# Third layer: mean first at the norms, reciprocal at once, bias columns two heads ahead, a values quarter in the first head

## What is computed

```python
def _cross_attention(q_in, kv_in, wq, bq, wk, bk, wv, bv, wo, bo, bias_k, bias_v):
    qh = (q_in @ wq + bq).reshape(b, q_len, H, K)
    kh = (kv_in @ wk + bk).reshape(b, t, H, K)
    vh = (kv_in @ wv + bv).reshape(b, t, H, K)
    kh = jnp.concatenate([kh, jnp.broadcast_to(bias_k, (b, 1, H, K))], axis=1)
    vh = jnp.concatenate([vh, jnp.broadcast_to(bias_v, (b, 1, H, K))], axis=1)
    logits = jnp.einsum('bqhk,bthk->bhqt', qh, kh) / scale
    weights = jax.nn.softmax(logits, axis=-1)
    ctx = jnp.einsum('bhqt,bthk->bqhk', weights, vh).reshape(b, q_len, H * K)
    return ctx @ wo + bo

res = x
h = _layer_norm(x, ln1_scale, ln1_offset)
x = res + _cross_attention(h, xf_1, wq1, ...)
res = x
h = _layer_norm(x, ln2_scale, ln2_offset)
x = res + _cross_attention(h, xf_2, wq2, ...)
h = _layer_norm(x, ln_mlp_scale, ln_mlp_offset)
h = jax.nn.gelu(h @ w_fc1 + b_fc1, approximate=False) @ w_fc2 + b_fc2
return x + h
```

## Time and profile before

| what | us |
|---|---|
| timed runs, median of 3 (lowest, highest) | 5109.34 (5104.77, 5110.42) |
| the profiled execution | 5106.48 |
| its span, first to last instruction | 5104.8 |
| busy in the span: TensorE, its weight loads | 4528.8, 3317.1 |
| busy: VectorE, ScalarE, GpSimd | 3084.9, 1932.5, 1675.9 |

### The profile page before, as it was taken

How to read it: one execution, slowest core, us unless ns; L and a number is a source line. 1 busy time by engine, 2 the same in 40 slices (tenths; PEclk the granted TensorE clock), 3 DMA queues, 4 the chain that set the end, 5 groups by cost and what they waited for, 6 DMA issues and landing times. The chain is left out here.

```text
span 5104.8 us, 72497 instructions
## 1 busy us (share of the span) xinstructions
PE 4528.8 (89%) x22864; PEld 3317.1 (65%) x22864; DVE 3084.9 (60%) x6414; ACT 1932.5 (38%) x3756; POOL 1675.9 (33%) x1119
## 2 busy tenths in 40 slices
PE   6999999578888888659999999998998999999996
PEld 3444444355666666448878778787787876877874
DVE  4555555147666666627677477575675756757642
ACT  2444444212222222125545245453354542545521
POOL 1222232235444444312323433323323234233240
PEclk8999988778888998779999999999999999999999
DMA  0000000200000000011211221211312112221123
GB/s 35 22 26 17 17 21 9 95 5 9 13 13 13 13 9 1 17 60 59 62 61 58 71 86 55 74 59 58 96 55 74 59 61 83 63 67 53 53 70 113
DMA packets 126288, 240.90 MB, mean 47 GB/s; under 512 B 16884, under 2 KB 38132, under 8 KB 124896
## 3 DMA queue, kind: packets, MB, share of 16 engines
q1 hardware_dynamic: 123744, 229.50, 14.2%
q0 software_dynamic: 2304, 8.39, 0.4%
HBM read 220.79 MB, written 16.78 MB: 47 GB/s over the span
## 5 line engine op out<-in xcount | busy, mean ns | idle before, releaser
L1786 POOL TENSOR_TENSOR c_wl<-c_wr,c_wh 128x512 fp32r<-128x512 f32 (+1 forms) x576 | 822.1, 1431 | 1744.8 <-ACT c_wh L2107 1531.7
L2199 ACT ACTIVATE c_pr<-c_ps,c_nms 128x257 f32<-128x257 f32 x512 | 245.3, 479 | 577.6 <-DVE c_nms L2389 575.1
L1355 POOL TENSOR_TENSOR b_sb<-b_sb,b_rt 128x1024 f32<-128x1024 f32 x128 | 285.0, 2227 | 490.1 <-DVE b_sb L1395 490.1
L572 ACT ACTIVATE a_ex<-a_ps 128x1024 f32<-128x1024 f32 x256 | 261.7, 1025 | 345.9 <-PE a_ps L408 345.6
L1395 DVE TENSOR_TENSOR_SCAN b_sb<-b_wt,b_s,b_ps 128x256 f32<-128x256 f32 x512 | 356.0, 732 | 11.7 <-issue 3.9
L1850 PE MATMUL c_ps<-c_hh,c_wh 128*128 128x512 f32 x768 | 319.4, 416 | 49.1 <-POOL c_hl L1792 49.1
L666 DVE TENSOR_REDUCE a_nm<-a_ps 128x2 f32<-128x1024 f32 x256 | 310.8, 1219 | 76.0 <-PE a_ps L385 73.0
L1850 PE MATMUL c_ps<-c_gh,c_wh 128*128 128x512 f32 x768 | 312.4, 407 | 41.9 <-DVE c_kl L2328 31.9
L2107 ACT ACTIVATE c_wh<-c_wr 128x512 fp32r<-128x512 f32 (+1 forms) x464 | 315.3, 685 | 9.6 <-PE c_ps L1852 8.5
L1852 PE MATMUL c_ps<-c_hh,c_wl 128*128 128x512 f32 x768 | 313.1, 408 | 0.0
L1851 PE MATMUL c_ps<-c_hl,c_wh 128*128 128x512 f32 x768 | 312.6, 407 | 0.0
(11 more groups left out here) (307 smaller groups left out, 11007.7 us busy)
## 6 DMA issues: line engine op xcount, KB each, us to landing
c_wr<-in_downs SPq DMA_DIRECT2D x192, 256.0 KB, 2.6
c_wr<-in_wv SPq DMA_DIRECT2D x64, 512.0 KB, 3.9
c_wr<-in_wk SPq DMA_DIRECT2D x128, 256.0 KB, 2.7
c_wr<-in_wq SPq DMA_DIRECT2D x128, 256.0 KB, 2.6
c_wr<-in_fc SPq DMA_DIRECT2D x64, 256.0 KB, 2.8
b_w<-in_w SPq DMA_DIRECT2D x8, 1024.0 KB, 13.5
a_x<-in_x SPq DMA_DIRECT2D x8, 512.0 KB, 3.4
a_ctx<-in_ctx SPq DMA_DIRECT2D x8, 512.0 KB, 4.1
```

What stands on the lines that cost most here:

```text
L572: act.activation(EX[:, n % 4, :, :], ps[:, BT + 2 * (n % 2):BT + 2 * (n % 2) + 2, :], ACT.Exp).then_inc(ex_ready, 1)
L1355: pool.tensor_tensor(SB[:, quad % 3, :, 0:L], SB[:, quad % 3, :, 0:L], RT[:, scan % 2, q // 4, :].unsqueeze(1).broadcast_to([P, 4, L]), AL ...
L1786: pool.tensor_tensor(piece(WL, slot), piece(WR, slot), piece(WH, slot), ALU.subtract).then_inc(piece_cut[slot], 1)
L2199: act.activation(PR[:, i, 0:L + 1], ps[:, BS + 1 - i % 2, 0:L + 1], ACT.Exp, bias=NMS[:, i:i + 1], scale=float(K2) ** -0.5, accum_out=RS[: ...
```

## The change

- *Norms.* TensorE: mean first, quarter 0, variance, quarters 1 and 2 (before: quarter 0, mean, quarter 1, variance, quarters 2 and 3). Quarter 3 stays in the norm only for attentions 2, 4 and 6 (`late_value` is true for 0, 1, 3, 5, 7); for the others it moves into head 0, between the next keys and queries and the transposes. VectorE: the reciprocal and the scaling come directly behind quarter 0, the low halves of quarters 1 and 2 behind the scaling. ScalarE: squares before the copy of quarter 0, the deviation before that of quarter 1, that of quarter 2 behind the high copies.
- *Columns.* `COL` has four slots instead of two, and the copy for head N + 2 is made in head N, behind the rows, instead of the copy for head N + 1 behind the softmax weights.
- *Ends of attentions.* `GL` of heads 0 and 1 is made by VectorE, one in head 14 and one in head 15, behind the rows, instead of both by GpSimd in head 14. TensorE's first output product waits for each of its banks just before it writes there, instead of for all three at first.
- *Feed-forward.* The next norm's reciprocals and scalings come one chunk earlier (after chunks 10 to 13 instead of 11 to 14).

```diff
-        COL = sb("col", [P, 2, 4])
+        COL = sb("col", [P, HSTEP, 4])
...
+        def late_value(t):
+
+            return t == 0 or t % 2 == 1
...
                 def head(h4, c, at=None):
                     u, v = c % 2, c // 2
-                    if at == H2 - 2:
-                        for m in range(2):
-                            pool.wait_ge(g_high, t * H2 + m + 1 + AHEAD)
-                            pool.sem_inc(passed, 1)
-                            pool.tensor_tensor(GL[:, m, :], G[:, m, :], GH[:, m, :], ALU.subtract).then_inc(g_low, 1)
...
             def gap(t, n):
 
-                if n == 0:
-                    pe.wait_ge(consts_in, 6 * 16 + AHEAD)
-                    pe.sem_inc(passed, 1)
-                    mean(n)
+                mean(n)
                 if t < B:
                     first_values(t, 0)
-                if n > 0:
-                    mean(n)
+                variance(n)
                 if t < B:
                     first_values(t, 1)
-                variance(n)
-                if t < B:
                     first_values(t, 2)
-                    first_values(t, 3)
+                    if not late_value(t):
+                        first_values(t, 3)
...
+                    if at == 0 and late_value(t):
+                        first_values(t, 3)
                     turn(N)
                     if at == H2 - 2:
 
-                        pe.wait_ge(v_low, t * H2 + H2 + AHEAD)
-                        pe.wait_ge(q_low, N + 2 + AHEAD)
-                        pe.wait_ge(k_low, N + 2 + AHEAD)
-                        pe.sem_inc(passed, 1)
                         down_ready(0)
-                        for d in (2, 0, 1):
+                        for d, free, count in ((2, v_low, t * H2 + H2), (0, q_low, N + 2), (1, k_low, N + 2)):
+                            pe.wait_ge(free, count + AHEAD)
                             add_down(0, DOWN_BANKS, 0, d, True)
...
                 act.wait_ge(g_used, used_count(last, 14) + AHEAD)
                 cut(1, count)
                 cut(0, count)
+                squares(n)
                 first_values(t, 0)
-                squares(n)
+                deviation(n)
                 first_values(t, 1)
-                deviation(n)
-                first_values(t, 2)
                 act.wait_ge(d_ps, n * EC + AHEAD)
                 act.sem_inc(passed, 1)
                 cut(3, count)
                 cut(2, count)
-                first_values(t, 3)
                 norm_high(n, range(EC))
+                first_values(t, 2)
+                if not late_value(t):
+                    first_values(t, 3)
...
-            def columns(N, index, u):
...
+            def columns(N, index, s):
-                dve.wait_ge(c_ready, N - 1 + AHEAD)
+                dve.wait_ge(c_ready, N - HSTEP + 1 + AHEAD)
                 dve.sem_inc(passed, 1)
-                dve.tensor_copy(COL[:, u, :], HC[:, index, :]).then_inc(col_ready, 1)
+                dve.tensor_copy(COL[:, s, :], HC[:, index, :]).then_inc(col_ready, 1)
...
             def gap(t, n):
-                first_values(t, 0)
                 centered(n)
                 if n % 3 == 1:
                     first_columns(t)
+                first_values(t, 0)
+                inverse(n, slice(0, N2))
+                scaled(n, range(EC))
                 first_values(t, 1)
                 first_values(t, 2)
-                inverse(n, slice(0, N2))
-                scaled(n, range(EC))
...
                             rows(N, t * (H2 // 2) + h4 * 2 + v, u)
+                            if at is None or at < H2 - 2:
+                                columns(N + 2, a * H2 + h4 * 4 + c + 2, (c + 2) % HSTEP)
+                            else:
+                                context_low(at - (H2 - 2))
...
                     if at != H2 - 1:
+                        queries(N + 1, (c + 1) % HSTEP)
                         if at != 0:
-                            columns(N + 1, a * H2 + h4 * 4 + c + 1, 1 - u)
-                        queries(N + 1, 1 - u)
-                        if at != 0:
-                            keys(N + 1, 1 - u)
+                            keys(N + 1, (c + 1) % HSTEP)
...
+                            if n == 10:
+                                inverse(b * 3 + 3, slice(0, L))
                             if n == 11:
-                                inverse(b * 3 + 3, slice(0, L))
+                                inverse(b * 3 + 3, slice(L, N2))
                             if n == 12:
-                                inverse(b * 3 + 3, slice(L, N2))
+                                scaled(b * 3 + 3, range(0, 2))
                             if n == 13:
-                                scaled(b * 3 + 3, range(0, 2))
-                            if n == 14:
                                 scaled(b * 3 + 3, range(2, 4))
```

More of the change, by code:

```diff
@@ L2420, in head, with context_low @@
                            .then_inc(pt_low, 1)
-                head_steps(t, dve, head)
-                for n in range(2, H2):
+                def context_low(n):
                     dve.wait_ge(g_high, t * H2 + n + 1 + AHEAD)
```

52 lines of the change are left out of this document (31 added, 21 removed).

## The result

The changed kernel takes 4966.55 us (median of 4 runs, 4958.13 to 4975.81) against 5108.73 (4 runs, 5104.77 to 5110.42) beside it: a ratio of 0.9723, 95% interval 0.9702 to 0.9744. It is 142 us faster; the forecast was 87, with a range down to 5000. The profiled execution took 4961.53 us with a span of 4959.9 (before: 5106.48 and 5104.8). The direction and the mechanism of most seams were right, the size was not: 55 us were missed, because the middle heads, held to be bound by TensorE, were not.

A forecast was written before the change was run, and what follows sets the result against it. The prediction took TensorE to bound the middle heads, so only seams could pay: 35 + 24 + 17 + 5 + 3 + 3 = 87 us, from 5106.5 to 5019.5 profiled, 5022 for the timed runs. The range was 5000 to 5056.

The forecast's parts named there:

- the first paragraph: Middle heads of an attention: bound by TensorE, busy 79.3 of 80 us, so only the seams can pay.
- G: Column copy in the 112 heads: 0.2 us on VectorE beside a never idle TensorE, so 0 gained.
- A: Heads 14 and 15 of the eight attentions: earlier low keys, part given back in head 15; 35 us gained.
- The third rival: Slower: the moved column copy meets GpSimd in every head, up to 128 us lost, total 5150; chance 0.03.
- the first rival: Head 15's late second low context brings half clock, so heads 14 and 15 gain 19 us, total 5038; chance 0.12.
- B: Norm between the two attentions of a pair, four times: mean first and an earlier reciprocal; 24 us gained.
- C: Norm before the feed-forward, three times: same steps with all four quarters kept; 17 us gained.
- F: End of the feed-forward, three times: scaling one chunk earlier frees VectorE for the last low half; 3 us gained.
- D: Start of the third layer, once: earlier deviation and cut, quarter 3 off the path to the first keys; 5 us.
- E: First three heads of the eight attentions: earlier columns gain 3 us in three, quarter 3 in head 0 nets 0 in five.
- The worst bound of the sum: Whole kernel: all bounds at their worst give 53 us gained, a total of 5056.
- What would show it: Profile signs: head 14's low-key wait gone, 1.5 to 2 in head 15, reciprocal 10.3 after mean, no ScalarE column waits.

The follow-up runs named there:

- experiment 7: The changed kernel with one VectorE instruction (low half of a values piece) made twice in heads 2 to 14, 0.75 us more a head: 4977.71 us.
- Experiments 1 and 2: 1: the kernel before with only the column copy changed, 5019.29 us; 2: the changed kernel with the column copy put back, 5041.5 us.
- 6: The kernel before with one VectorE instruction (low half of a values piece) made twice in heads 2 to 14, 0.75 us more a head: 5178.9 us.
- Experiment 8: The changed kernel with quarter 3 ahead of head 0's exponentials, the second low context ahead of head 15's rows, GpSimd's cuts behind the norm's low halves: 4957.87 us.
- experiment 12: The changed kernel with the two low contexts made by GpSimd again, bank-wise waits kept: 4971.16 us.
- Experiment 9: The changed kernel with only GpSimd's cuts moved behind the norm's low halves, in the seven norms that follow an attention: 4958.51 us.
- experiment 11: The changed kernel with quarter 3 in the norm for all eight attentions, the rest as changed: 4972.96 us.
- norms-alone kernel: The kernel before with only the norms changed, including quarter 3 in head 0 and the feed-forward scalings one chunk earlier: 5072.69 us.
- experiment 10: The kernel of Experiment 9, with GpSimd's cuts in heads 0 and 1 also waiting for VectorE's softmax weights of the extra key: 4954.99 us.

## Why the prediction was right or wrong

**What bounds the kernel (the first paragraph), and G.** This is the step that failed: the looped heads were taken as bound by TensorE and the copy in them priced at 0, where they gave 53 us, and a part of A more. "TensorE is busy 79.3 of 80 us" was taken to mean that it is never idle, so that nothing in front of it could pay. The share is that of instructions which overlap, and their modelled ends cover small gaps. Two views of the kernel before would have cast doubt on it: the weight loads wait for exponentials 13 times in ten heads, and none of VectorE's waits there names TensorE (a sign that experiment 7 shows to be weak alone). Experiments 1 and 2 price the step at 52 and 50 us, 6 and 7 show which engine set the pace. The third rival named the very condition, "from the point where VectorE's chain is longer than TensorE's head, that is, if its 17 idle us in 80 lay elsewhere than on this chain", and gave it 0.03 as a loss. The condition held; the sign was wrong, because the same edit took a wait of 1.5 out of that chain and put 0.15 back: 124 of the 128 copies behind the rows took 0.16 and met no GpSimd, four took 1.2.

**A (35; 52).** The mechanism was right: the low-key wait in head 14 is gone, and one of 1.42 stands in head 15. Two sizes were off. Head 14 lost 7.3, of which 0.5 is the looped heads' gain; and the price in head 15 was 0.3 to 0.5 in seven attentions and 3.0 in one, 0.74 on the mean, instead of the 1.6 (6.0 less 4.4) taken off for a wait of 1.5 to 2.0. The wait came with 1.34 to 1.51. Experiment 8 shows why it cost less: it lies beside VectorE's chain and costs nothing itself. The 3.0 of attention 5 is VectorE's chain behind GpSimd's cuts, a price that the prediction didn't have. The net of 1.3 for taking the contexts from GpSimd was right (experiment 12). Half of A, the first rival, did not happen.

**B (24; 13.5), C and F (20; 13.2).** The order of steps came as forecast, the size was off. The reciprocal starts 10.67 after the mean, 10.3 was forecast, so 0.4 of the 2.6 missed per norm in B is here. The term that was mis-sized is the 0.9 taken off for GpSimd beside the scaling: from the reciprocal's start to the last low half it took 12.65 before and takes 15.1, 2.45 more. Not one scale is stretched but two instructions of VectorE and then a low half of GpSimd, and the collision is carried from chunk to chunk. Experiment 9 takes these 2.4 us away and gets back 3.0 per norm (11.8 in four). What the prediction worked out from the rule of the Trainium skill (SBUF — State Buffer, section SBUF: two separate sides), 7 us less, was on the right side; it counted the first chunk alone, and B, C and F together missed 17. F has its own sign: the waits of 0.92, 0.92 and 1.20 at the end of the feed-forward are 0.67, 0.68 and 0.67, so that 1 us came of the 3.

**D (5; 5.3)** was right, with 3 of it from quarter 3 (experiment 11). The wait for the cut stands as before (4.36), and the cut comes 0.7 earlier after the first mean, 0.9 was forecast.

**E (3; 5.6).** Head 1 gained 8.1 by the columns, as experiment 1 has it with 7.2, more than was forecast; heads 0 and 1 grew by 5.2 in the norms-alone kernel. That quarter 3 is neither gained nor lost within the attentions holds. The worst bound of the sum took -5 for E without the 3 of attentions 2, 4 and 6; with them it is 56 instead of 53, far from what was measured either way.

**What would show it.** The signs for A, B and C and for the columns were seen, the new wait a little below its 1.5; of the heads 0 of the odd attentions those of 3 and 7 are as long as before, those of 5 and 1 are 1.1 and 1.8 longer. The last sentence, "the seams are as short as forecast and the total isn't", is what happened, in the good direction.

## What to carry to other kernels

A busy share near 100% doesn't show that an engine is the bound when its instructions overlap: look for its own short waits, those of its weight loads too, and count its instructions. Here the weight loads waited 13 times in ten heads before and not once after. Where another engine's waits never name it, that is a hint and no more; what settles it is to make that other engine longer by a known piece and see whether the loop grows by it. Two engines that take turns in a ring can set the pace at 78% and 55% busy; there a wait between them counts in full, every round, and an instruction that nobody waits for counts little. And before a wait is priced, follow the engine that ends it: if it is busy without a gap to the end of the stage, removing the wait moves it and saves nothing.

## What was not expected of the hardware

A lower clock made a head shorter. Head 0 of attention 2 is the same code in the changed kernel and in experiment 8. Windows view from just ahead of the exponentials' wait to the transposes, of the changed kernel, then of experiment 8:

```profile
2941.00:2947.00 6.00, 5.60 (x21) 4.50 (x22) 4.94 (x20) 2.56 (x9) 0.78 (x1) 0.72 0.60 195
```

```profile
2941.50:2947.50 6.00, 5.08 (x26) 3.86 (x26) 4.95 (x20) 3.52 (x11) 0.80 (x1) 1.00 0.63 201
```

The head took 10.54 us with the clock granted at 0.72 and 11.51 with 1.00. The timeline of the first:

```profile
2946.22 1.27 POOL L1790 TENSOR_TENSOR c_wl<-c_wr,c_wh 128x512 fp32r<-128x512 f32 x1 [11.90 <-ACT c_wh L2102]
2946.24 1.27 DVE L2405 CAST c_pbh<-c_pr 128x4 fp32r<-128x4 f32 x1
2947.59 0.16 DVE L2407 TENSOR_TENSOR c_pb<-c_pr,c_pbh 128x4 f32<-128x4 f32 x1
```

and of the second:

```profile
2946.70 2.50 POOL L1790 TENSOR_TENSOR c_wl<-c_wr,c_wh 128x512 fp32r<-128x512 f32 x2 [11.90 <-ACT c_wh L2104]
2946.72 1.27 DVE L2409 CAST c_pbh<-c_pr 128x4 fp32r<-128x4 f32 x1
2948.07 1.15 DVE L2411 TENSOR_TENSOR c_pb<-c_pr,c_pbh 128x4 f32<-128x4 f32 x1
...
2949.45 0.28 PE L1934 MATMUL c_ps<-c_id,c_pb 128*12 128x128 f32 x1 [2.11 <-DVEq L2414]
```

At full clock the queries are done earlier, ScalarE's second cut with them, and GpSimd makes two cuts in a row instead of one. Two of VectorE's small instructions stand behind GpSimd then, and TensorE waits 2.11 for them. The traces of the other kernels show the same step, experiment 10 apart, where GpSimd waits for VectorE there: a head 0 without quarter 3 takes 10.5 to 10.9 where 0.72 is granted in the 6 us behind the wait of 2.24, and 11.45 to 11.9 where 1.00 is. In the kernel before it is four attentions of each kind, and the 2.10 of the earlier trace rows stands in exactly the four with 1.00; there head 1 gives most of it back (12.7 to 13.1 behind a long head 0, 12.9 to 13.5 behind a short one). In the changed kernel attentions 2, 4 and 6 have 0.72 and in experiment 9 they have 1.00, which is the 5.5 us in heads 0 and 1 that it gave back. With quarter 3 in head 0 it is the other way round: 12.0 to 12.3 with 0.72, 11.5 to 11.9 with 1.00, because TensorE then has more to do at the lower clock. What decides whether the clock falls there was not tried.
